# A two-layer graph network on one core: the second layer's routing logits move from TensorE to VectorE

## The reference

```
z = relu(layernorm(x))
for l in range(2):
    weights = softmax(z @ envW[l] + envb[l])           # [N, 4]: the logits of this text
    agg = scatter_mean(z[col], row)                    # mean over the edges into each node
    combined = concat([agg, z], axis=-1)               # [N, 512]
    outputs = einsum('nd,kdo->nko', combined, W[l]) + z[:, None, :]
    z = relu(einsum('nk,nko->no', weights, outputs))
out = x + z
```

## Time and profile before

| | |
|---|---|
| median of three runs | 1713.21 us (1709.35 to 1716.23) |
| the profiled execution's own time | 1716.39 us |
| its span, first to last instruction | 1714.3 us |
| TensorE matmul busy | 1542.7 us, 90% |
| VectorE busy | 880.7 us, 51% |
| ScalarE busy | 576.5 us, 34% |
| GpSimd busy | 1216.0 us, 71% |
| mean granted TensorE clock | 0.975 |

### The profile page before, as it was taken

The page is one execution under the profiler, slowest core; times in us unless marked ns, Lnnn a source line. Parts: engine busy times, 40 slices in busy tenths (PEclk is TensorE's granted clock), DMA queues, the critical chain, the costliest instruction groups (busy, mean ns, idle before and its releaser), DMA issues. The chain is left out here.

```text
span 1714.3 us, 35546 instructions
## 1 busy us (share of the span) xinstructions
PE 1542.7 (90%) x8502; PEld 1111.2 (65%) x8503; DVE 880.7 (51%) x2029; ACT 576.5 (34%) x1254; POOL 1216.0 (71%) x1187
## 2 busy tenths in 40 slices
PE   1149999999999999999992599999999999999998
PEld 1036767777777777767770476777777766677776
DVE  6673666666666666666651144433444444434433
ACT  4413444444444444444440022222222222222222
POOL 1377777777777777777775377777777777776774
PEclk9998999999999999999995699999999999999999
DMA  7877777777777777777778877777777777777775
GB/s 216 288 225 214 223 227 224 218 208 216 223 224 211 218 218 226 223 206 217 221 217 312 309 234 239 239 237 236 228 232 233 235 233 230 233 232 224 239 231 158
DMA packets 160202, 393.34 MB, mean 229 GB/s; under 512 B 36989, under 2 KB 61080, under 8 KB 160180
## 3 DMA queue, kind: packets, MB, share of 16 engines
q0 software_dynamic: 92544, 302.70, 60.0%
q10 hardware_dynamic: 35112, 61.46, 9.9%
q1 hardware_dynamic: 32524, 28.91, 5.4%
HBM read 347.61 MB, written 45.37 MB: 229 GB/s over the span
## 5 line engine op out<-in xcount | busy, mean ns | idle before, releaser
L712 POOL DMA_INDIRECT ring<-zp_dram,gather_idx x1152 | 1197.8, 1040 | 411.7 <-issue 261.2
L1379 PE MATMUL agg_ps<-zp,stage 128*128 128x258 f32 x1568 | 447.8, 323 | 10.6 <-PEq L101 10.6
L1341 PE MATMUL agg_ps<-ring,onehot 128*128 x1248 | 383.0, 337 | 30.8 <-PEq L101 25.5
L1412 PE MATMUL mix_ps<-w_sb,turned_z 128*128 128x512 f32 x784 | 400.9, 611 | 0.0
L1412 PE MATMUL mix_ps<-w_sb,turned_m 128*128 128x512 f32 x784 | 390.8, 598 | 0.5 <-PEq L101 0.5
L1381 PE MATMUL agg_ps<-zp,stage 128*128 128x256 f32 x1568 | 384.5, 281 | 0.0
L1105 ACT ACTIVATE stage<-counts_sb 128x512 fp32r<-128x512 uint8 (+1 forms) x416 | 248.8, 605 | 371.4 <-ACTq L101 370.5
L1379 PEld LDWEIGHTS agg_ps<-zp,stage 128*128 128x128 f32 x1568 | 295.9, 189 | 72.2 <-issue 68.4
L1346 PE MATMUL agg_ps<-ring,onehot 128*128 x1248 | 322.5, 287 | 0.0
L1381 PEld LDWEIGHTS agg_ps<-zp,stage 128*128 128x128 f32 x1568 | 296.3, 189 | 35.0 <-issue 35.0
L1341 PEld LDWEIGHTS agg_ps<-ring,onehot 128*128 128x128 f32 x1248 | 242.1, 194 | 71.4 <-issue 68.7
(11 more groups left out here) (159 smaller groups left out, 901.2 us busy)
## 6 DMA issues: line engine op xcount, KB each, us to landing
ring<-zp_dram,gather_idx POOLq DMA_INDIRECT x1152, 3.8
zp_dram<-zp SPq DMA_DIRECT2D x7, 1792.0 KB, 7.1
a_dram<-counts_sb ACTq DMA_DIRECT2D x16, 784.0 KB, 4.6
zp_dram<-parts ACTq DMA_DIRECT2D x49, 256.0 KB
zp<-zp_dram SPq DMA_DIRECT2D x4, 1792.0 KB, 38.3
counts_sb<-a_dram ACTq DMA_DIRECT2D x17, 400.0 KB
parts<-in_x ACTq DMA_DIRECT2D x48, 128.0 KB
counts_sb<-a_dram ACTq DMA_DIRECT2D x16, 384.0 KB
```

The source lines that it names most:

```text
L712: pool.indirect_dma_start(out=ring[:, k, t, 0:2 * D].bitcast(F32), out_offset=None, in_=zp_dram[l], in_offset=bass.IndirectOffsetOnAxis(ap ...
L1341: mm = pe.matmul(agg_ps[:, bank, 0:D + 2], onehot[:, place, t, :], rows[:, :, D:2 * D + 2], start=place == 0 and t == 0, stop=True, skip_g ...
L1379: pe.matmul(agg_ps[:, bank, 0:D + 2], stage[:, g % 2, i, :], zp[:, c, D:2 * D + 2], start=c == 0, stop=True, skip_group_check=True)
L1412: mm = pe.matmul(mix_ps[i][:, :], (turned_z, turned_m)[what][:, c, :], w[:, i * HALF:(i + 1) * HALF], start=what == 0 and c == 0, stop=wha ...
```

## The change

For layer 2 the eight weight columns' worth of `envW[1]` are spread once over all partitions: VectorE writes each column chunk on the diagonal of a [128, 128] tile, and TensorE multiplies an all-ones matrix with these, which leaves envW's values repeated on every partition in the two `win_ps` banks (no longer needed after layer 1). From then on VectorE computes each logit itself as one `scalar_tensor_tensor` over 256 columns, `z_in` times one spread column, with the sum over the row as accumulator output. So `logits_of` has no matmul in layer 2, and `take_logits` does nothing there. `own_logits` stands behind the one-hots in the dense slot (for that slot's own block), behind `keep_z` in the dense slot (for the short slot's block) and behind `result` in the short slot (for the first slot's block). `keep_z`, in both layers, now settles on its add and signals s_zin by an instruction of its own.

```diff
                     def keep_z(blk):
                         whole = zp[:, bass.ds(blk, 1), :]
-                        nc.vector.tensor_tensor(z_in[:], whole[:, :, 0:D].bitcast(F32),
-                                                whole[:, :, D:2 * D].bitcast(F32), ALU.add).then_inc(s_zin, 1)
+                        settle(nc.vector.tensor_tensor(z_in[:], whole[:, :, 0:D].bitcast(F32),
+                                                       whole[:, :, D:2 * D].bitcast(F32), ALU.add))
+                        dve.sem_inc(s_zin, 1)
...
+                    def spread_weights(l):
+
+                        take(dve, s_keyfree[1])
+                        nc.vector.memset(all_ones, 1.0)
+                        for k in range(K):
+                            for c in range(DC):
+                                ins = nc.vector.tensor_scalar(diagonals[k][:, c * P:(c + 1) * P], ident[:],
+                                                              envw_sb[:, l, c, k:k + 1], None, ALU.mult)
+                        ins.then_inc(s_diag, 1)
+
+                    def own_logits(l):
+
+                        dve.wait_ge(s_spread, 1)
+                        for k in range(K):
+                            ins = nc.vector.scalar_tensor_tensor(
+                                out=terms[k], in0=z_in[:], scalar=1.0, in1=logit_weights(k),
+                                op0=ALU.mult, op1=ALU.mult, accum_out=logits[:, k:k + 1])
+                        settle(ins)
+                        settle(nc.vector.tensor_tensor(logits[:], logits[:], bias[:, l * K:(l + 1) * K], ALU.add))
+                        nc.vector.tensor_reduce(negmax[:], logits[:], AX.X, ALU.max, negate=True).then_inc(s_nmax, 1)
+
                     def take_logits(l):
+                        if l:
+                            return
...
                         if not first:
+                            spread_weights(l)
                             dve.wait_ge(s_zload[0], 16)
                         keep_z(0)
+                        if not first:
+                            own_logits(l)
...
                                     compare_next(lo, hi, 0)
+                                    if not first:
+                                        own_logits(l)
...
                                 keep_z(block_of(dve, r, dn, k + 1))
+                                if not first and k == DENSE_AT:
+                                    own_logits(l)
...
                                 if not first:
                                     result()
+                                if not first and k == PER_ROUND:
+                                    own_logits(l)
...
+                    def spread_weights():
+                        for p in range(2):
+                            take(pe, s_wfree[p])
+                        take(pe, s_diag)
+                        for k in range(K):
+                            for c in range(DC):
+                                mm = pe.matmul(logit_weights(k)[:, c * P:(c + 1) * P], all_ones,
+                                               diagonals[k][:, c * P:(c + 1) * P], start=True, stop=True,
+                                               skip_group_check=True)
+                        mm.then_inc(s_spread, 1)
+
                     def logits_of(l):
                         take(pe, s_Tz)
-                        take(pe, s_lgfree)
-                        for c in range(DC):
-                            mm = pe.matmul(lg_ps[:, 0:K], turned_z[:, c, :], envw_sb[:, l, c, :], start=(c == 0),
-                                           stop=(c == DC - 1))
-                        mm.then_inc(s_logit, 1)
+                        if l == 0:
+                            take(pe, s_lgfree)
+                            for c in range(DC):
+                                mm = pe.matmul(lg_ps[:, 0:K], turned_z[:, c, :], envw_sb[:, l, c, :], start=(c == 0),
+                                               stop=(c == DC - 1))
+                            mm.then_inc(s_logit, 1)
                         pe.wait_ge(s_w[l], 16 * CC)
```

More of the change, by code:

```diff
@@ L210, in gnn_kernel @@
         s_logit = sem("logits_ready")
+        s_diag = sem("logit_weights_on_diagonals")
+        s_spread = sem("logit_weights_spread")
         s_lgfree = sem("logits_taken")
@@ L647, in gnn_kernel, with logit_weights @@
             stage = mb("stage", [P, 2, STAGE, P], F32R)
+            all_ones = win_lo[:].rearrange("p v n -> p (v n)")[:, 0:2 * P].bitcast(F32)
+            terms = [win_lo[:].rearrange("p v n -> p (v n)")[:, 2 * i * D:2 * (i + 1) * D].bitcast(F32) for i in range(3)]
+            terms.append(lg_ps[:, 0:D])
+            some = win_lo[:].rearrange("p v n -> p (v n)")[:, 2 * P:2 * P + 2 * (K - 1) * D].bitcast(F32)
+            diagonals = [some[:, k * D:(k + 1) * D] for k in range(K - 1)] + [mean[:]]
+            assert 2 * P + 2 * (K - 1) * D <= 2 * max(PAIRS_IN) * P and K == 4 and K * D // 2 <= 512
+            def logit_weights(k):
+                return win_ps[k // 2][:, (k % 2) * D:(k % 2 + 1) * D]
             def rounds_of(eng):
@@ L1550, in _ @@
                             pe.sem_inc(s_free[l], RU)
+                            spread_weights()
                         turn_z()
```

## The result

The changed kernel takes 1716.29 us, the median of 11 runs (1714.46 to 1720.44). The kernel before took 1712.66 us in 11 runs beside them (1709.35 to 1716.23). The ratio is 1.0026, with a 95% interval of 1.0014 to 1.0037. The forecast was 1733 us, in a range from 1712 to 1747. So the change costs 3.6 us where 20 were expected. The ratios leave out one execution of experiment 9, which took 2266.99 us at a granted clock of 0.667.

A forecast was written before the change was run, and what follows sets the result against it. Layer 2 was taken to alternate between a VectorE, ScalarE and DMA chain and TensorE, with layer 1's short slots on VectorE. Layer 1 +16, layer 2 +4.2, -0.7 and +0.5, together +20 us: 1733 us, range 1712 to 1747.

The forecast's parts named there:

- TensorE's removed matmuls: Layer 2 logit matmuls: only the dense slot's end counts, gaining 0.36 us per round, about 0.7 in the first.
- The settle in layer 1: keep_z: 1.2 us of register work no longer hidden under the add; 1.3 us per round, 16 us in all.
- The slacks of the first slot's turn: Layer 1, between z_in's end and its turn: 0.47 us of slack in five rounds, absorbing 2.3 us.
- The settle in layer 2: keep_z of the short slot: register work starts 0.64 us later, shifting the chain to the counts one for one.
- The exponential: Layer 2 logits' chain: starts 0 to 0.1 us sooner behind its reduction; 0.1 us per round taken.
- The work added: Layer 2 multiplications, settle, bias add, reduction: 2.9 us per block, 3.0 us of room behind result; 0.1 us per round added.
- rival 3: Logits behind the result take their upper bound, counts 0.9 us late: 12 us more, 1745 us; chance 0.11.
- The spreading: Weights spread at the layer boundary, covered by VectorE's 20.67 us wait for reloaded rows: cost 0, about 5 us once without cover.
- The counts' landing: Layer 2, from the counts' issue to the dense slot's first stage fill: taken as unchanged, no term.
- The boundary: Between layer 1's end and layer 2's start: no term, so layer 1's delay passes it unchanged.

The follow-up runs named there:

- experiment 9: Changed kernel with look_ahead cut in two, its plan load and register work moved ahead of keep_z's wait and add: 1716.05 us, ratio 1.0007.
- experiment 7: Changed kernel with the two logit matmuls of each layer 2 block still issued, into columns nobody reads: 1727.55 us, ratio 1.0077.
- experiment 8: Changed kernel with the four multiplications and a settle run twice behind the result in each round's last short slot: 1739.78 us, ratio 1.0148.
- second profiles: The kernel before and the changed kernel run once more, both unchanged: 1711.72 us and 1718.44 us.
- experiment 2: Changed kernel with keep_z's settle in layer 2 alone, layer 1 as before: 1709.19 us, ratio 0.9977.
- experiment 5: experiment 3's kernel with SyncE's 16 pairs of takes ahead of the reload replaced by one wait for each count: 1695.05 us, ratio 0.9885.
- experiment 6: Kernel before with only SyncE's 16 pairs of takes ahead of the reload replaced by one wait for each count: 1705.51 us, ratio 0.9948.
- experiment 4: Changed kernel with the reload of kept rows held back until layer 1's last store has landed: 1724.01 us, ratio 1.0056.
- experiment 1: Kernel before with only keep_z's settle and separate semaphore instruction added, in both layers: 1724.29 us, ratio 1.0071.
- experiment 3: Changed kernel with the settle only where the multiplications follow, in layer 2's first block and the dense slot: 1703.12 us, ratio 0.9941.
- experiment 10: experiment 5's kernel with the look_ahead cut of experiment 9: 1700.84 us, ratio 0.9909.

## Why the prediction was wrong

Point by point, by its own steps:

- **TensorE's removed matmuls**, 0.36 us for one block a round: the place was right, the size small. Two ways measured 0.45 (24.43 to 23.98) and 0.49 (experiment 7). In experiment 7 more than that came back, through the counts.
- **The settle in layer 1**, +16: right. +14.7 in the changed kernel, +14.8 with the settle alone, and the middle round is 1.3 us longer as foreseen. The mechanism is the one told: with the register work moved ahead of the add (experiment 9) `nodes` stands 0.48 us behind it instead of 1.73, so 1.25 us of the 1.54 are that work. The slacks of the first slot's turn were used up. `nodes` came later than the forecast's 1.4 us, since the load from `plan` took 0.49 us on the mean behind the add and 0.31 ahead of it.
- **The settle in layer 2**, 0.64 us a round: measured 0.46. The load from `plan`, 0.56 us in the earlier trace rows, took 0.47 us on the mean of 16 short slots before and takes 0.31 behind the add, which is most of the difference.
- **The exponential**, 0.1 us sooner: right, 0.39 to 0.28.
- **The work added**: no delay of the reciprocal against the exponential (0.53 and 0.54 us), where 0.1 was taken; the copy of the mean ahead of it came 0.08 us later behind the result. The block is 2.12 us, not 2.9, as the reads of the accumulator lie beside the next multiplication. But the room was not 3.0 us either, it was 2.5. Two errors against each other; rival 3 was 0.4 us away, as experiment 8 shows.
- **The spreading**, 0: the cover named was gone. The first reloaded rows had landed at 926.6 while the nine operations ran (925.97 to 927.58), and the first block's multiplications then waited 3.6 us for TensorE's eight matmuls. TensorE's first product waited for the weights until 964.22, so another cover lay behind; whether the spreading cost anything was not tried.
- **The counts' landing**, taken as unchanged: 0.44 us a round sooner, 6.6 us in all, the larger part of layer 2's error.
- **The boundary**, for which the sum has no term, so that layer 1's delay passes it unchanged: this is the step that failed first. It returned 8.4 us (5 to 8 by the second profiles), shown by experiment 2, where half of layer 1's gain was lost again. That the reload's place does it is shown by experiments 5 and 6, and by experiment 4 in part: held back, the reload took 2 to 5 us of the 8.4 away again.

So +16, +4 and nothing at the boundary became +14.7, -7.3 and -8.4. The largest term and its cause were right; the forecast fell on a stretch that it had not costed, and on a DMA's landing. That the measured time still lies inside the stated range is no credit to the working: it stands near the lower end, and layer 1 absorbed no more of the delay than foreseen.

The Trainium skill, "VectorE: DVE Perf Modes", section "The DRAIN you can't avoid", has semaphores cost nothing extra behind a row of Vector instructions (its advice to save instructions and not semaphores stands in the section "Rules for kernel authors"). No run here tests that for a row of such instructions, but at this place the settle cost 11.5 us (experiment 1). The same page, section "Two Vector instructions with no wait between them", counts an operation with accumulator output as two instructions; the trace agrees (the reads of 0.08 us), yet they add nothing to the distance of 0.34 us.

What stays open is why the counts land sooner in the changed kernel. The settle in layer 2's last short slot goes with a part of it: the eight profiles that have it there show 4.65 to 4.92 us, the six others 4.84 to 5.23. No single part gives all of it: the settle alone gives 4.75 us, the kernels of experiments 2 to 8 from 4.74 to 4.97, experiment 10 5.23, and rounds within one execution run from 3.4 to 6.2. It often moves against a change in when they are issued, but experiment 8 breaks that rule.

## What to carry to other kernels

A wait for the engine's own result costs more than its 0.2 us where the sequencer has register work to do next: put it only where the result is read, which was worth 13 us here (1716.3 to 1703.1). When a stage is made longer or shorter, cost the boundary behind it as well: ask of every transfer there what it hangs on, because one that does not hang on the stage's end keeps its place, and issuing the reload sooner was worth 8 us. What the boundary waits for then is layer 2's weights, and no run moved their load. And when work is moved ahead on an engine that sets the time, look at which engine comes next: in layer 1 GpSimd already issued its gathers without a pause.

## What the runs showed of the hardware

GpSimd's gather instruction takes 0.94 to 0.97 us by itself, but up to 2.94 us when it begins just as VectorE compares window keys (bf16 from f16, 1960 columns, 2.19 us). In layer 1 of the kernel before, 150 to 870 us, the longest was 2.32 us, and 128 gathers that overlapped a compare of the windows (`win_key` or `win_lo`) took 1.45 us on the mean, 380 others 1.00. In the changed kernel 13 took over 2.5 us, in experiment 9 15, in experiment 5 none. The Trainium skill, "Trainium Architecture — The Big Picture", section "What this means for kernel authors", says that VectorE and GpSimd share a pair of ports under an exclusive lock; the trace agrees so far as the gather of 571.22 ends 0.8 us behind the end of the compare. No run here tried another number type for the keys.

The load from `plan` by VectorE's sequencer has no fixed price. In the 16 short slots of layer 2 it took 0.30 to 0.73 us where it started under the add, and 0.30 to 0.34 us behind it in the changed kernel. In layer 1 it was the other way round: 0.30 to 0.31 us ahead of the add, under VectorE's key compare, and 0.30 to 0.64 us behind the add, with VectorE idle. What sets it stays open.
